# Edge blocks in groups of eight instead of four, six densely summed ranges instead of five, and shorter stages, in a graph network kernel on one core

## The chip, the core and the metric

The kernel runs on one core of a Trainium2 chip. The metric is the device time in microseconds (us) of one execution. The kernel before took 3231.09 us, the median of three runs that lay between 3231.09 and 3231.75 us.

Engines by the names of the profile: PE multiplies matrices and PEld loads its weights, DVE is the vector engine, ACT the scalar engine, POOL is GpSimd, and SP only starts transfers. A q behind a name (SPq) is that engine's own sequencer or transfer queue.

## What is computed

Two layers of a mean-aggregating graph convolution on 12500 nodes with 256 features and 200000 edges, then a third product, the residual and a layer normalization. The edges come sorted by dst, and dst is skewed: it is 12500 times the square of a uniform number, so low node numbers have many edges and high ones few.

```
def _sage_conv(x, src, dst, W_l, b_l, W_r):
    agg = segment_sum(x[src], dst, 12500)
    deg = segment_sum(ones, dst, 12500)
    mean = agg / maximum(deg, 1)[:, None]
    return mean @ W_l + b_l + x @ W_r
h = relu(_sage_conv(x, src, dst, W1_l, b1, W1_r))
h = relu(_sage_conv(h, src, dst, W2_l, b2, W2_r))
out = layernorm(x + h @ W3 + b3)
```

Layer 2 first multiplies h by W2_l and stores the product as z_rows; its gather reads z_rows, as that of layer 1 reads in_x.

## The kernel before, in words

The edges are cut into 1563 blocks of 128. The nodes are cut into 100 ranges of 125 (WN), and the sums of each range have a column block of `acc` in SBUF. Two methods fill the sums.

**Gathered blocks.** All blocks from number 348 (HB) on, 1216 of them, are gathered in each layer: POOL starts one indirect transfer per block (L446), which fetches 128 rows of 256 numbers into `ring`, 4 slots (R) of 4 blocks (GB). For each group of 4 blocks DVE makes a one-hot matrix `oh` by comparing the int16 columns `dcol` with the int16 `iota` (`mark_group`, L1013, 128x500 results), PE multiplies it with the rows (`product`, L538, four products that add into one PSUM bank of three), and DVE adds the bank twice into `acc`, each time with a mask, since a group may touch two neighbouring ranges (`add_masked`, L970). Where a group's node numbers span 125 or more, `later_pass` repeats compare, product and adds; with four blocks no group does. The order of the groups takes one from the low end and one from the high end in turn. POOL waits before the first block of a group for the third product of the group four before it (s_gr), and before its last block for that of the next group.

**Dense ranges.** The first 348 blocks hold nearly all edges of the first 5 (HW) ranges. They aren't gathered. DVE and PE count edges per pair of source and destination node instead: `chunk` makes two one-hot matrices for a pair of blocks (L1063, L1066), PE multiplies them (L589), and DVE copies the counts out (`keep_counts`, L1104). A range has 25 such chunks, and the counts go to HBM (`counts`). Then PE multiplies the counts with all rows of x in 20 steps of 5 products (`dense_step`, L615), and DVE adds two steps at a time to `acc` (`add_hot`, L1120). SP loads counts and rows of each step into two places (`load_step`). A range whose edges lie in the first blocks only in part is also served by `fallback`: 20 steps per layer that load the same rows again and do work only where such a range exists past the dense ones. In this trace none does, and a step there is two small DVE instructions (L1132, L1135), a handshake and its loads.

**Order of the work.** It is written out by hand on each engine, in loops of `four` groups. Layer 1: 4 groups, the table of spans (`spans`), a stage of 48 groups that counts range 0 (a chunk after every second group), four stages of 48 groups that count range w and in their last ten fours run the 20 dense steps of range w-1, two fours with fallback steps, ten fours with the dense steps of range 4, three more fours with fallback steps. Layer 2 has no counting: fallback steps first, then five stages of dense steps, then fours without. Between the groups each finished range of 125 nodes goes through the dense layers (`dense1`, `dense2`, called tiles here), at most one per two groups (`finish_one`). Tables that tell each group's range, offset, passes and finished ranges are computed on DVE, PE and ACT at the start, before the first group.

Of the kernel before, what the change touches and what calls it, by code (L numbers as in the profile page):

```python
# [23 lines left out]
P = 128  # L24
WN = 125
NW = N // WN
GB = 4
# [12 lines left out]
HW = 5  # L40
HB = 348
# [3 lines left out]
C0 = T0 * P  # L45
NC = (NT - T0) * P
G0 = HB // GB
NGG = NG - G0
KJ = (N + P - 1) // P
# [17 lines left out]
TW = 4 * (HW * CH + 1)  # L67
BANKS = 3
STAGE = 48
TAIL_GROUPS = NGG - 4 - STAGE * (HW + 1) - STEPS + 8  # L70
assert STEPS == 4 * PARTS and CD * CH == WN and 2 * FG >= CH and TAIL_GROUPS == 0
# [8 lines left out]
def hot_end(w):  # L80

    return 4 + STAGE * (w + 1) + STAGE

# [18 lines left out]
C_MA = C_BS + HW * CH  # L102
# [7 lines left out]
def constants():  # L110
# [12 lines left out]
    d = np.zeros((HW * CH, D_N), np.float32)  # L123
# [4 lines left out]
    k = np.arange(HW * CH)  # L128
    d[:, D_LIM] = CD * turned
    d[:, D_LIM + 1] = CD * turned + CD - 1  # L130
    d[:, D_LIM + 2] = WN * k
    d[:, D_LIM + 3] = WN * k + WN - 1
# [10 lines left out]
    rows = np.zeros((HW * CH + 1, 4), np.int32)  # L143
# [15 lines left out]
def build(nc, x, src, dst, W1l, b1, W1r, W2l, b2, W2r, W3, b3, c_f, c_s, c_win, c_node, out):  # L159
# [5 lines left out]
    with ExitStack() as ctx:  # L165
# [6 lines left out]
        def sem(name):  # L172
            return ctx.enter_context(nc.semaphore(name))

        acc = sb("acc", [P, (NW + 2) * RW])
        ring = sb("ring", [P, R, GB, RW])
        scol = sb("scol", [P, NC], I32)
        dcol = sb("dcol", [P, NC], I16)
        oh = sb("oh", [P, R, GB, WN])
# [19 lines left out]
        NH = HW * CH  # L199
        tables = sb("tables", [65, NGG * 4], I32)  # L200
        tab = tables[0:1, :]
# [10 lines left out]
        psA, psD = ps4[:, 0:BANKS * 512], ps4[:, BANKS * 512:]  # L212
# [18 lines left out]
        few = scratch[:, u + SJ * WN:u + 2 * SJ * WN].rearrange("p (j n) -> p j n", j=SJ)  # L231
# [4 lines left out]
        cs = scratch[0:NH, u:u + D_N]  # L236
# [10 lines left out]
        span = scratch[0:NH, u:u + 6]  # L247
        u += 6
        m1 = scratch[0:NH, u:u + HB]
# [9 lines left out]

        ident, resid, wt, bs, upper, lower = (cf[:, a:a + n] for a, n in (  # L260
            (C_ID, P), (C_RES, WN), (C_WT, NW), (C_BS, NH), (C_MA, WN + 1), (C_MB, WN + 1)))
# [23 lines left out]
        s_fall = [sem("s_fall0"), sem("s_fall1")]  # L285
# [14 lines left out]
        credit = {s_mm[0]: 4, s_mm[1]: 4, s_ad[0]: 1, s_ad[1]: 1, s_T: 1, s_tc: 1, s_h: 1, s_z: 2,  # L300
# [9 lines left out]
        def _(sp):  # L310
# [17 lines left out]
            tail(1, dst, s_e3)  # L328
            edges(0, src, 0, T0, s_e4)
            sp.dma_start(cs, c_s).then_inc(s_nd, 16)  # L330
            sp.dma_start(iota[:], c_node.to_broadcast([P, NI])).then_inc(s_w, 16)
# [26 lines left out]
            users = [0]  # L358
            last_use = [0, 0]

            def place(q):

# [1078 lines left out]
```

## Time and profile before

| | before |
|---|---|
| median of 3 runs | 3231.09 us |
| the profiled execution's own time | 3232.92 us |
| its span | 3231.0 us |
| PE busy | 2516.2 us (78%) |
| POOL busy | 2368.5 us (73%), 2439 instructions |
| DVE busy | 1483.5 us (46%) |
| ACT busy | 497.8 us (15%) |
| moved by DMA | 651.35 MB, mean 202 GB/s |
| granted PE clock, mean | 0.919 |

The span is what the profiler covers from the first to the last instruction; the execution's own time has 1.9 us around it. POOL is busy for its 2432 gathers and a handful of small instructions. Its busy share is 0.7 to 0.8 of nearly every slice, and the rest of those slices is idle time between two gathers.

### The profile page before, as it was taken

The page shows a single profiled execution, that of the slowest core. Times are in us where ns is not written, and L with a number is a line of the kernel's source. Part 1 is how long each engine was busy: PE and PEld are TensorE (multiplying, and loading weights), DVE is VectorE, ACT ScalarE, POOL GpSimd, SP SyncE. Part 2 cuts the span into 40 slices and gives each one's busy share as a digit, 9 for nine tenths or more (in the row PEclk, how much of TensorE's full clock was granted, in tenths as well). Part 3 has the DMA queues.
Part 4 walks back from the last instruction along what each step waited for, and adds up shares of the span by engine and source line. Part 5 has one row for each costly group of instructions (what it writes and reads, how often), then busy time and mean ns, then how long its engine had stood idle before and what let it go on. Part 6 is the DMA issues. An engine that isn't in the chain of part 4 may idle for free.

```text
span 3231.0 us, 55773 instructions
## 1 busy us (share of the span) xinstructions
PE 2516.2 (78%) x11663; PEld 2060.8 (64%) x11664; DVE 1483.5 (46%) x3552; ACT 497.8 (15%) x1511; POOL 2368.5 (73%) x2439
## 2 busy tenths in 40 slices
PE   4777888888888888687756678878878868877776
PEld 2545677677677677576644556767757757756655
DVE  6777656665655655433333333333333333333332
ACT  2001110101111111110101121112112212211113
POOL 4767777777777777777747777777777777777775
PEclk9989999999999999899978889989989989989978
DMA  4435687687687687777745667757757757757743
GB/s 120 132 115 160 206 251 238 203 254 239 193 256 247 201 255 243 239 219 216 227 147 175 189 193 224 214 169 232 219 171 225 223 171 229 222 174 224 220 121 108
DMA packets 495880, 651.35 MB, mean 202 GB/s; under 512 B 184223, under 2 KB 414230, under 8 KB 492564
## 3 DMA queue, kind: packets, MB, share of 16 engines
q0 software_dynamic: 116736, 318.92, 33.1%
q1 hardware_dynamic: 298228, 254.51, 25.7%
q10 hardware_dynamic: 80800, 76.82, 7.8%
q14 instruction: 98, 0.80, 0.1%
q8 instruction: 18, 0.29, 0.0%
HBM read 579.62 MB, written 70.41 MB: 201 GB/s over the span
## 4 chain that ended last, share of the span: by engine, by line
POOL 40%; issue 20%; PE 19%; DMA 9%; DVEq 7%; DVE 5%; ACT 1%; SPq 0%; ACTq 0%; PEldq 0%; PEld 0%; POOLq 0%
POOL ring L446 40%; PE ps L538 11%; DMA ring<-z_rows,scol 5%; PE ps L615 3%; DMA ring<-in_x,scol 2%; DVEq L990 1%; DVE acc L970 1%; PE psY L659 1%; PE psB L589 1%; DVE oh L1066 1%; DVE oh L1013 1%; PE psY L692 1%; PE psY L648 1%; DVEq L970 1%; PE psT L706 1%
## 5 line engine op out<-in xcount | busy, mean ns | idle before, releaser
L538 PE MATMUL ps<-ring,oh 128*125 128x257 f32 (+1 forms) x4864 | 1332.7, 424 | 547.5 <-DMA ring<-z_rows,scol 286.3
L446 POOL DMA_INDIRECT ring<-in_x,scol x1216 | 1188.1, 977 | 432.1 <-issue 357.7
L538 PEld LDWEIGHTS ps<-ring,oh 128*125 128x125 f32 x4864 | 973.1, 208 | 810.0 <-issue 657.2
L446 POOL DMA_INDIRECT ring<-z_rows,scol x1216 | 1179.8, 970 | 403.6 <-issue 354.3
L970 DVE SCALAR_TENSOR_TENSOR acc<-ps,cf,acc x1224 | 535.6, 479 | 654.4 <-PE ps L538 420.6
L1013 DVE TENSOR_TENSOR oh<-dcol,iota 128x500 f32 x608 | 414.5, 682 | 308.3 <-issue 235.5
L615 PE MATMUL ps<-scratch 128*125 128x257 f32 (+1 forms) x2000 | 490.5, 393 | 11.4 <-DMA scratch<-counts 7.7
L615 PEld LDWEIGHTS ps<-scratch 128*125 128x125 f32 x2000 | 465.6, 296 | 35.0 <-DMA scratch<-counts 8.1
L1363 ACT ACTIVATE work<-psT,b2c 128x125 f32<-128x125 f32 x200 | 62.0, 362 | 1190.5 <-PE psT L710 1190.5
L1327 ACT COPY work<-psY 125x256 f32<-125x256 f32 x100 | 37.2, 372 | 1244.8 <-PE psY L648 1244.8
L589 PE MATMUL psB<-oh 128*128 (+1 forms) x546 | 161.4, 393 | 84.0 <-DVE oh L1066 78.4
L1120 DVE TENSOR_TENSOR acc<-ps,acc 125x256 f32 (+2 forms) x100 | 42.5, 425 | 377.4 <-PE ps L615 364.4
L659 PEld LDWEIGHTS psY<-work,w 128*128 128x128 f32 x1600 | 198.3, 195 | 7.3 <-issue 1.1
L1066 DVE TENSOR_SCALAR oh<-iota,cf,key 128x500 int16 (+1 forms) x546 | 201.1, 410 | 0.0
L659 PE MATMUL psY<-work,w 128*128 128x125 f32 x1600 | 197.7, 277 | 0.8 <-issue 0.8
L589 PEld LDWEIGHTS psB<-oh 128*128 (+1 forms) x546 | 49.7, 97 | 178.0 <-issue 150.8
L648 PE MATMUL psY<-w,hT 128*125 128x256 f32 x400 | 112.5, 406 | 18.4 <-issue 16.9
L706 PE MATMUL psT<-hT,w 128*128 x800 | 121.6, 274 | 0.0
L1063 DVE TENSOR_TENSOR oh<-iota,key 128x256 int16 (+1 forms) x273 | 113.9, 417 | 12.2 <-PE psB L589 10.1
L706 PEld LDWEIGHTS psT<-hT,w 128*128 128x128 f32 x800 | 113.2, 191 | 6.1
L692 PE MATMUL psY<-w,work 128*125 128x256 f32 x400 | 110.6, 401 | 5.3 <-issue 2.8
L1180 DVE RECIPROCAL rs<-sd 125x1 f32 (+1 forms) x100 | 16.4, 164 | 205.5 <-ACT sd L1388 180.0
(139 smaller groups left out, 1211.0 us busy)
## 6 DMA issues: line engine op xcount, KB each, us to landing
scratch<-counts SPq DMA_DIRECT2D x200, 312.5 KB
scratch<-in_x SPq DMA_DIRECT2D x114, 512.0 KB
scratch<-z_rows SPq DMA_DIRECT2D x114, 512.0 KB
counts<-scratch SPq DMA_DIRECT2D x25, 1250.0 KB
work<-in_x ACTq DMA_DIRECT2D x200, 125.0 KB
ring<-in_x,scol POOLq DMA_INDIRECT x1216
ring<-z_rows,scol POOLq DMA_INDIRECT x1216, 3.7
scratch<-in_x SPq DMA_DIRECT2D x114, 128.0 KB
```

The lines of the kernel that those rows point to most:

```text
L446: pool.indirect_dma_start(ring[:, slot, b, 0:D], None, rows_dram, bass.IndirectOffsetOnAxis(scol[:, n - C0:n - C0 + 1], 0)).then_inc(rows[ ...
L538: mm = pe.matmul(psA[0:WN, bass.ds(bank, W)], oh[:, slot, b, :], ring[:, slot, b, 0:W], start=(b == 0), stop=(b == nb - 1))
L589: mm = pe.matmul(psB[:, 0:n], oh1[:, bass.ds(at, P)], oh1[:, bass.ds(at + P, n)], start=first and b == 0, stop=True, skip_group_check=True)
L615: mm = pe.matmul(psD[0:WN, 0:W], lin_a[:, q, :, :, k].rearrange("p f n -> p (f n)"), lin_x[:, q, k, 0:W], start=(q == 0 and k == 0), stop= ...
L648: mm = pe.matmul(psZ[0:WN, 0:D], hT[:, k * WN:(k + 1) * WN], w2[:, k, 0:D], start=(k == 0), stop=(k == 1))
L659: mm = pe.matmul(psH[:, m * WN:(m + 1) * WN], w1[:, a, k, m * P:(m + 1) * P], tT[:, 2 * a + k, :], start=(a == 0 and k == 0), stop=(a == 1 ...
L692: pe.matmul(at, tT[:, k, :], w3[:, k, :], start=(k == 0), stop=False)
L706: pe.matmul(psT[:, m * WN:(m + 1) * WN], w2[:, k, D + m * P:D + (m + 1) * P], hT[:, bass.ds(q + k * WN, WN)], start=(k == 0), stop=False)
L970: ins = v.scalar_tensor_tensor(out=to, in0=psA[0:WN, bass.ds(bank, W)], scalar=mask[0:WN, bass.ds(k, 1)], in1=to, op0=ALU.mult, op1=ALU.add)
L1013: v.tensor_tensor(to, cols, at, ALU.is_equal).then_inc(s_oh[l], 1)
L1063: v.tensor_tensor(s[:, :, 0:P], iota[:, 0:P].unsqueeze(1).to_broadcast([P, 2, P]), key[:, 0, bass.ds(at, 2)].unsqueeze(2).to_broadcast([P, ...
L1066: ins = v.tensor_scalar(s[:, b, P:P + n], iota[:, table:table + n], base, key[:, 1, bass.ds(at + b, 1)], ALU.add, ALU.is_equal)
```

## The change

Groups are 8 blocks (GB = 8, in two ring halves of 4), so each is one compare of 128x1000 results and one pair of masked adds for 8 blocks. The first 376 blocks are not gathered (six dense ranges), which leaves 149 groups, 1192 gathers, per layer. `oh` has 2 buffers of 8 blocks, and `acc` products go to 2 PSUM banks. PE's group is two half products, each waiting for its own 4 blocks, with a dense step placed between the halves. A stage is 11 bodies of two groups. The loop without counts ahead of stage 0 is one body (AHEAD = 1), and no tile is finished in it. The fallback steps (now `general_step`) reuse the rows that the dense steps of the last range (layer 1) or the first range (layer 2) have loaded. The start is reordered: the first group runs before the rest of the tables, the keys and the weight loads.

```
-GB = 4
+GB = 8
+HALF = 4
-HW = 5
-HB = 348
+HW = 6
+HB = 376
-BANKS = 3
-STAGE = 48
+BODIES = NGG // 2
+STAGE = 11
+AHEAD = BODIES - STAGE * HW - 7
-        oh = sb("oh", [P, R, GB, WN])
+        oh = sb("oh", [P, 2, GB, WN])
...
# SP: order at the start, and the loads of the general steps
+            sp.dma_start(cs, c_s).then_inc(s_nd, 16)
+            sp.dma_start(iota[:], c_node.to_broadcast([P, NI])).then_inc(s_io, 16)
...
             edges(0, src, 0, T0, s_e4)
-            sp.dma_start(cs, c_s).then_inc(s_nd, 16)
-            sp.dma_start(iota[:], c_node.to_broadcast([P, NI])).then_inc(s_w, 16)
...
-                if w == HW - 1:
-                    fallback(x, 2, 8)
...
-                    load_step(x, w, t)
+                    load_step(x, w, t, w == HW - 1)
-                if w == HW - 2:
-                    fallback(x, 0, 2)
-            fallback(x, 8, STEPS)
-            fallback(z_dram, 0, STEPS)
# POOL
-                    slot = g % R
                     for b in range(GB):
-                        if g >= R and b == 0:
-                            pool.wait_ge(s_gr[l], g - R + 1)
-                        if g >= R and b == GB - 1:
-                            pool.wait_ge(s_gr[l], g - R + 2)
+                        half, slot = b // HALF, (g + 1) % 2 * 2 + b // HALF
+                        if g >= 2 and b % HALF == 0:
+                            pool.wait_ge(s_gr[l], 3 * (g - 2) + (3 if half else 1))
+                        if g >= 2 and b == HALF - 1:
+                            pool.wait_ge(s_gr[l], 3 * (g - 2) + 2)
+                        if g >= 2 and b == GB - 1:
+                            pool.wait_ge(s_mm[l], credit[s_mm[l]] + g - 1)
# PE
+            def group(l, i, between=()):
...
+                half_product(l, i, 0)
+                for work_ in between:
+                    work_()
+                pe.wait_ge(rows[l][2 * i + 1], landed)
+                half_product(l, i, 1)
...
+                    first_group()
+                    turn_tables()
+                    turn_keys()
...
+                    with pe.Fori(0, AHEAD):
+                        body(finishes=False)
+                    turn_spans()
+                    count()
+                    body(counts=2)
+                    with pe.Fori(0, STAGE - 1):
+                        body(counts=1)
+                    with pe.Fori(1, HW):
+                        count()
+                        body(counts=2)
+                        with pe.Fori(0, STAGE - 1):
+                            body(counts=1, steps=even)
+                    with pe.Fori(0, 3):
+                        body(steps=((0,), (1,)), after=((), (0,)), general=True)
+                        body(steps=((1,), (1,)), after=((0,), ()), general=True)
+                    body(steps=even, general=True)
# DVE
-                mark_group(l, i, nb, off)
+                mark_group(l, i, off)
...
-                add_product(l, i, *(behind[i] if i < 2 else row_of(i - 2)[0:2]))
+                if not first:
+                    add_product(l, 1 - i)
```

On DVE, in the plain groups at the start of layer 1, the rows of one group of four blocks read, with oh the one-hot matrix and acc the sums:

```order
L1013 ISA [waits s_mm0]
L1013 TENSOR_TENSOR oh<-dcol,iota 128x500
L990 ISA
L990 TENSOR_LOAD tables
L976 ISA
L970 ISA [waits s_ad0,s_mm0]
L970 ISA
L970 SCALAR_TENSOR_TENSOR acc<-ps,cf,acc 125x257
L970 ISA
L970 SCALAR_TENSOR_TENSOR acc<-ps,cf,acc 125x257
```

and those of one group of eight blocks:

```order
L1019 ISA [waits s_mm0]
L1019 REGISTER_ALU
L1019 TENSOR_TENSOR oh<-dcol,iota 128x1000
L1051 ISA
L1000 ISA
L1000 TENSOR_LOAD tables
L1001 ISA
L986 ISA [waits s_ad0,s_mm0]
L986 SCALAR_TENSOR_TENSOR acc<-ps,cf,acc 125x257
L986 ISA
L986 SCALAR_TENSOR_TENSOR acc<-ps,cf,acc 125x257
```

The compare has twice the results; the adds keep their size and stand once per eight blocks.

On PE, in a counting stage of layer 1, a group before and the dense step (its operand is scratch) behind it:

```order
L538 ISA [waits s_ad0,s_oh0]
L538 MATMUL ps<-ring,oh 125x257 x4
L543 ISA
L552 TENSOR_LOAD tables
L571 ISA
L604 ISA [waits s_dbank]
L615 MATMUL ps<-scratch 125x257 [waits s_lin0]
L615 MATMUL ps<-scratch 125x257 x4
```

and the same place now:

```order
L543 MATMUL ps<-ring,oh 125x257 [waits s_ad0,s_oh0]
L543 MATMUL ps<-ring,oh 125x257 x3
L607 ISA
L601 ISA [waits s_dbank]
L612 MATMUL ps<-scratch 125x257 [waits s_lin0]
L612 MATMUL ps<-scratch 125x257 x4
L543 MATMUL ps<-ring,oh 125x257 [waits rows0_1]
L543 MATMUL ps<-ring,oh 125x257 x3
```

The dense step has moved from behind a whole group to between its halves.

## Rows read from the trace of the kernel before

**Rows 1.** The costliest groups of the page: line engine op | busy, mean ns | idle before.

```profile
L446 POOL DMA_INDIRECT ring<-in_x,scol x1216 | 1188.1, 977 | 432.1 <-issue 357.7
...
L446 POOL DMA_INDIRECT ring<-z_rows,scol x1216 | 1179.8, 970 | 403.6 <-issue 354.3
L970 DVE SCALAR_TENSOR_TENSOR acc<-ps,cf,acc x1224 | 535.6, 479 | 654.4 <-PE ps L538 420.6
L1013 DVE TENSOR_TENSOR oh<-dcol,iota 128x500 f32 x608 | 414.5, 682 | 308.3 <-issue 235.5
```

**Rows 2.** Line L446: durations ns min/median/max, first and last start, then idle.

```profile
L446 POOL DMA_INDIRECT ring<-z_rows,scol x1216: 942/946/1452, 1654.9 to 3203.8; - x174
...
  issue: 712.0, 2337
```

**Rows 3.** Timeline of POOL, gathers behind a wait: start, us, engine, line [idle before].

```profile
49.62 1.18 POOL L446 DMA_INDIRECT ring<-in_x,scol  x1 [20.31 <-PE ps L538]
...
73.64 0.94 POOL L446 DMA_INDIRECT ring<-in_x,scol  x1 [5.34 <-PE ps L538]
...
190.88 0.94 POOL L446 DMA_INDIRECT ring<-in_x,scol  x1 [14.41 <-PE ps L538]
213.86 1.02 POOL L446 DMA_INDIRECT ring<-in_x,scol  x1 [3.02 <-PE ps L538]
...
1379.31 0.94 POOL L446 DMA_INDIRECT ring<-in_x,scol  x1 [9.54 <-PE ps L538]
...
1620.43 0.94 POOL L446 DMA_INDIRECT ring<-in_x,scol  x1 [3.17 <-PE ps L538]
1654.85 0.94 POOL L446 DMA_INDIRECT ring<-z_rows,scol  x1 [33.48 <-DMA z_rows<-work]
```

**Rows 4.** Timeline of POOL and DVE, three gathers near a compare, in pairs.

```profile
1657.30 0.68 DVE L1013 TENSOR_TENSOR oh<-dcol,iota 128x500 f32 x1 [0.60 <-issue]
1657.35 1.45 POOL L446 DMA_INDIRECT ring<-z_rows,scol  x1 [0.30 <-issue]
...
2630.54 0.95 POOL L446 DMA_INDIRECT ring<-z_rows,scol  x1 [0.31 <-issue]
2630.70 0.68 DVE L1013 TENSOR_TENSOR oh<-dcol,iota 128x500 f32 x1 [0.66 <-issue]
...
2635.29 0.68 DVE L1013 TENSOR_TENSOR oh<-dcol,iota 128x500 f32 x1
2635.54 1.24 POOL L446 DMA_INDIRECT ring<-z_rows,scol  x1 [0.30 <-PE ps L538]
```

**Rows 5.** Timeline of DVE, the widest instruction on two int16 operands, in the preparation.

```profile
33.13 1.43 DVE L877 TENSOR_TENSOR dcol<-dcol,scratch 128x1216 int16<-128x1216 int16 x1 [1.40 <-DMA scratch<-bounds]
```

**Rows 6.** Gathers per 80 us: stretch, length, POOL busy (count), PE clock, DMA share, GB/s.

```profile
0.00:80.00 80.00, 35.05 (x37) 0.91 0.44 120
80.00:160.00 80.00, 61.11 (x63) 0.91 0.44 130
160.00:240.00 80.00, 48.40 (x49) 0.87 0.39 118
240.00:320.00 80.00, 60.80 (x64) 0.98 0.52 158
```

**Rows 7.** Timeline of DVE and PE: first compare, one four of stage 0, its end.

```profile
45.59 0.68 DVE L1013 TENSOR_TENSOR oh<-dcol,iota 128x500 f32 x1 [4.25 <-issue]
...
89.85 0.68 DVE L1013 TENSOR_TENSOR oh<-dcol,iota 128x500 f32 x1 [1.45 <-issue]
...
99.71 3.74 PE L538 MATMUL ps<-ring,oh 128*125 128x257 f32 x16 [0.92 <-DVE oh L1013]
...
109.93 0.68 DVE L1013 TENSOR_TENSOR oh<-dcol,iota 128x500 f32 x1 [1.46 <-issue]
...
330.57 0.68 DVE L1104 COPY scratch<-psB 128x500 f32 x1 [2.11 <-issue]
```

**Rows 8.** All engines, the busiest 80 us of PE: PE, PEld, DVE, ACT, POOL busy.

```profile
480.00:560.00 80.00, 71.90 (x361) 59.73 (x360) 49.89 (x122) 8.81 (x25) 60.80 (x64) 0.98 0.80 252
```

**Rows 9.** Timeline: first dense step of range 4, and the last add of layer 1.

```profile
1372.73 4.66 PE L615 MATMUL ps<-scratch 128*125 128x257 f32 x10 [7.73 <-DMA scratch<-counts]
...
1634.29 0.88 DVE L970 SCALAR_TENSOR_TENSOR acc<-ps,cf,acc  x2 [0.33 <-DVE acc L970]
```

More of the change, by code:

```diff
@@ L781, in layer, with step, body @@
-                with pe.Fori(0, STEPS // 4 + (1 if l else -2)):
-                    four(general=(0, 1, 2, 3) if l == 0 else ())
+                def step(q, general):
+                    dense_step(l, q)
+                    if general:
+                        general_step(l, q)
+                def body(counts=0, steps=((), ()), after=((), ()), general=False, finishes=True):
+                    pe.reg_add(turn, turn, 16 * HALF)
+                    for i in range(2):
+                        group(l, i, [lambda q=q: step(q, general) for q in steps[i]] + [count] * (counts > 1))
+                        for q in after[i]:
+                            step(q, general)
+                        if counts:
+                            count()
+                        if finishes:
+                            finish_one(upto)
@@ L907, in _ @@
-            banks = [v.alloc_register(f"v_bank{k}") for k in range(BANKS)]
-            behind = [[v.alloc_register(f"v_{q}{k}") for q in ("at", "off")] for k in range(2)]
+            rows_at = [[v.alloc_register(f"v_row{k}_{q}") for q in ("w", "off", "passes", "done")] for k in range(2)]
+            behind, ahead = ([v.alloc_register(f"v_{q}_{a}") for a in ("w", "off")] for q in ("behind", "ahead"))
+            c, fin, ga, gb, extra, there, unit, upto = (
+                v.alloc_register(f"v_{q}") for q in ("c", "fin", "ga", "gb", "extra", "there", "unit", "upto"))
@@ L1193, in layer @@
                 v.reg_mov(ga, 0)
-                v.reg_mov(gb, 4 * (NGG - 2))
-                four_rows(front, ga)
+                v.reg_mov(gb, 4 * (NGG - 1))
+                for i in (1, 0):
+                    next_row(i)
                 v.reg_mov(c, 1)
-                for k in range(BANKS):
-                    v.reg_mov(banks[k], k * 512)
                 v.reg_mov(fin, 0)
-                for at, off in behind:
-                    v.reg_mov(at, NW)
-                    v.reg_mov(off, 0)
                 v.reg_mov(at_row, 0)
@@ new lines, in general_body @@
+                def general_body(w, first, second):
+                    for i, turns in enumerate((first, second)):
+                        group(l, i)
+                        for turn in turns:
+                            if turn == "general":
+                                general_step(l)
+                            else:
+                                summed(w)
+                        finish_one(upto)
+                if l == 0:
+                    group(l, 1, first=True)
+                    ends()
+                    keys()
+                    for i in range(2):
+                        v.reg_add((gb, ga)[i], (gb, ga)[i], (4, -4)[i])
+                        next_row(i)
+                    v.wait_ge(s_za, 8)
+                    with v.Fori(0, AHEAD):
+                        body(finishes=False)
@@ L1239, in layer @@
                     hot_chunk()
-                    with v.Fori(0, STAGE // 4):
-                        four(builds=True)
+                    body(counts=2)
+                    with v.Fori(0, STAGE - 1):
+                        body(counts=1)
                     with v.Fori(0, HW - 1) as w:
```

579 lines of the change are left out of this document (277 added, 302 removed).

## The prediction

> **What bounds the kernel now.** I read the page's costliest groups first, then the line of the gathers, then POOL's timeline for every gap over 0.31 us, and last what DVE does around those gaps. PE has the largest busy time, but it isn't the bound. POOL issues 2432 gathers of mean 977 and 970 ns [rows 1], median 946 [rows 2], and nearly every one follows the last after 0.30 us (712.0 us over 2337 gaps) [rows 2]. So a gather costs 1.25 us when nothing disturbs it, and 2432 of them are 3040 of the 3231 us. The reader is to see in the timeline how few real waits there are: 20.3, 5.3, 14.4, 3.0, 9.5 and 3.2 us in layer 1 and none in layer 2, and the 33.5 us between the layers [rows 3]. The rest is 8.9 us ahead of the first gather, 26 us behind the last (3203.8 [rows 2] to 3231.0), and about 70 us in which single gathers take longer than 946 ns: in layer 2, (970 - 946) ns x 1216 = 29.5 us.
>
> What makes a gather longer decides this change. The gather at 1657.35 began 0.63 us before the end of a compare and took 1.45 us; that at 2635.54 began 0.43 us before the end of one and took 1.24; that at 2630.54, in whose course a compare began, took 0.95 [rows 4]. So a gather that starts while DVE compares two int16 operands is held until 0.12 to 0.14 us before the compare's end, and one already running isn't touched. Layer 2 has no counting, so its 29.5 us over 304 compares put at most 0.097 us on a compare.
>
> The Trainium skill (SBUF — State Buffer, section "🔬 SBUF: two separate sides") says that VectorE with two SBUF inputs and GpSimd reading SBUF take an exclusive lock on a shared port pair, for the whole instruction. The trace bears out the hold and not its full extent: the compare at 2630.70 started inside a gather and still took 0.68 us. With the lock held for all of both instructions that compare would have been late; I go by the rows.
>
> **The change part by part.**
>
> Gathers: 1216 become 1192 per layer, 48 fewer at 1.25 us: -60.0 us.
>
> The longer compare: 128x500 takes 0.682 us [rows 1] and 128x1216 on two int16 operands 1.43 [rows 5], so 128x1000 takes 0.68 + 500/716 x 0.75 = 1.20 us. The hold grows faster than the length. If a compare of length T falls at any phase of the 1.275 us that a gather took in layer 2 ((3203.8 - 1654.9)/1215), the mean hold is (T - 0.12)²/(2 x 1.275): 0.123 us at T = 0.68, of which the trace has 79% (0.097), and 0.457 at 1.20, of which 79% are 0.36. I take 0.38. Bounds: 0.17 (growth with the length alone) and 0.46 (all phases alike). Layer 2: 149 compares, and 6 more because six groups of eight blocks span 125 nodes or more (groups 3, 5, 7, 9, 21 and 29 by the sorted dst), 155 x 0.38 = 58.9 against 29.5: +29.4. Layer 1 outside its first stage (there POOL waits for DVE, see below): 125 x 0.38 = 47.5 against 252 x 0.097 = 24.4: +23.1. Together +52.5 us.
>
> Counting: a sixth range has 32 pairs of blocks more (305 against 273), each with a small compare of the same kind; in layer 1 all of them cost (977 - 970) ns x 1216 = 8.5 us, so +1.
>
> The start and stage 0. Here DVE is the bound. One four takes it from 89.85 to 109.93, 20.1 us [rows 7], as long as 16 gathers; stage 0 runs from about 64 to 330.57 [rows 7], 266 us for 12 fours, 25 chunks and the sixteen pairs of the heaviest chunk, which cause the 14.4 us wait. In the new order a group of eight saves DVE one pair of adds (0.88), 0.16 of compare and about 0.2 of gaps, 2.5 us per body; 12 x 2.5 = 30 go, and with 11 bodies instead of 12 another 9 (what is left of a four without its chunks). The 25 chunks stay. New are four second passes in this stage (groups 3, 5, 7, 9): compare 1.2, eight products 3.7 [rows 7], adds 0.9 and handshakes, 7 us each in which DVE waits for PE: +28. Stage 0 thus takes 255 us. It does not begin earlier: the first compare comes at about 35 instead of 45.6 [rows 7], since its table is ready sooner, but then the rest of the tables, keys, one body and the spans follow, and the first chunk comes near 68 (before: 64). So the stage ends near 327, and the next compare lets POOL go on at about 334.5, after 216 gathers, with 976 to go. Before, 37 + 63 + 49 + 64 = 213 gathers were out at 320 [rows 6], 221 at 330.6, and 976 were left at 355. The lead is 20.4 us, where 24 gathers fewer are 30: +9.6. The body with four chunks that opens the next stage takes DVE some 24 us against 21 of POOL: +3. Error of this part by its rough steps: 10 us either way.
>
> Steady stages: before, PE is busy 71.9 of 80 us at its peak and POOL never waits [rows 3, 8]. Ten of eleven bodies instead of ten of twelve fours now carry dense steps; the peak within a body is the same and the slack of POOL is 14 blocks instead of 13. The dense step between the halves is hidden by the wait for the second four gathers (5 us). Cost 0, and 10 to 15 us if the cover goes.
>
> The late waits of layer 1, 9.5 and 3.2: the first came because SP had queued fallback loads ahead of the counts of range 4 [rows 9], and those loads are gone. What is late next is the store and reload of the last range's counts, which PE now meets in the first group after counting: I leave 3 us. -9.
>
> Between the layers: the last add came 13 us after the last gather [rows 3, 9], held up by the fallback handshakes; half a product and one pair of adds take 8. Three tiles still follow, before and now. -5 of the 33.5. The end of layer 2 stays.
>
> Sum: -60.0 + 52.5 + 1 + 9.6 + 3 - 9 - 5 = -7.9 us, against the profiled execution's own 3232.9: 3225.0. It lies 1.8 above the median of the runs, so the time comes to about 3223 to 3225: 3224.
>
> **The rivals.**
>
> A, the hold doesn't grow with the square. If a compare of 1.2 us costs a gather only in proportion (0.17), 280 compares cost 59 us less: 3165. For it: two gathers with a measured relation say nothing beyond 0.68 us. Against: nothing in the rows limits the hold, and 1.08 is still below the period.
>
> B, slower: DVE in stage 0. The second passes make DVE wait for PE while PE's rows, the chunk's banks and the spans wait for DVE. If body 1 with its four chunks and the passes run one after the other with PE at the low clock (eight products at 7 instead of 3.7 us) and the heavy chunk then meets an emptied ring, stage 0 takes 280 to 285 us instead of 255: 3250. It decides from the point at which a body takes DVE more than its 21 us of gathers over several bodies. For it: DVE has no idle in that stage already. Against: the group itself has become cheaper.
>
> C, the dense steps of the last range. 20 steps in 7 bodies instead of 10 fours, some only 5 us apart, with loads of 0.95 MB each, and the reload wait of 7.7 us seen before [rows 9]. If they come late and the shorter rest per stage no longer lets PE catch up, 12 to 16 us: 3238.
>
> D, the start pays off in full: stage 0 costs nothing against before: 3211.
>
> **How the numbers follow.** Forecast 0.50 (own range 3210 to 3240), A 0.15, B 0.20, C 0.10, D 0.05. A measurement of this kernel tells 0.2%, 6.5 us, from no change: faster is below 3224.6, slower above 3237.6. Of the forecast's 0.50, 0.27 is faster, 0.18 the same, 0.05 slower; A and D are faster; B gives 0.17 slower and 0.03 the same; C 0.04 and 0.06. That is 0.47, 0.27, 0.26. The range has to reach halfway into A and to the far side of B: 3178 to 3250.
>
> **What would show it.** In the new profile: 1192 gathers per layer with a median of 946 ns still and a mean near 1000 (970 + 24); compares of 1.20 us; gathers as long as 1.9 us. POOL's waits in layer 1: about 9 and 7 us before 60 us, 30 to 40 us in stage 0, then almost none; layer 2 as long as before, near 1550 us from first to last gather, although it has 24 gathers fewer. It is wrong if the mean gather stays at 975 (A), if the waits before 340 us exceed 75 (B), or if POOL waits in layer 2 at all.

## The result, and the profile of the changed kernel

The changed kernel takes 3302.59 us, the median of four runs (3302.32 to 3305.06), against 3231.09 (four runs beside it, 3229.62 to 3231.75): a ratio of 1.022, 95% interval 1.0206 to 1.0234. The forecast was 3224, range 3178 to 3250. It was wrong, in the sign and by more than its range. The profiled execution took 3302.32 us with a span of 3300.5, 69.5 more than before.

POOL is still the bound. The page's groups, line engine op | busy, mean ns | idle before, against those of [rows 1]:

```profile
L452 POOL DMA_INDIRECT ring<-in_x,scol x1192 | 1197.8, 1005 | 467.4 <-issue 340.3
L452 POOL DMA_INDIRECT ring<-z_rows,scol x1192 | 1184.6, 994 | 419.6 <-issue 343.7
...
L986 DVE SCALAR_TENSOR_TENSOR acc<-ps,cf,acc 125x257 f32 (+1 forms) x620 | 271.9, 480 | 747.7 <-PE ps L543 598.7
L1019 DVE TENSOR_TENSOR oh<-dcol,iota 128x1000 f32 x298 | 359.0, 1205 | 283.3 <-issue 188.2
```

Fewer gathers, but each 24 to 28 ns longer in the mean, and more idle time before them. The two lines of L452 alone, as in [rows 2]: min, median and longest gather, first and last start.

```profile
L452 POOL DMA_INDIRECT ring<-in_x,scol x1192: 940/946/1960, 8.8 to 1665.3; - x199
L452 POOL DMA_INDIRECT ring<-z_rows,scol x1192: 940/946/1975, 1701.4 to 3269.6; - x199
...
  issue: 683.9, 2244
  PE ps L543: 160.4, 138
```

The median is as before and so is the rhythm of undisturbed gathers (946 + 300 ns). The longest is 1.975 us in place of 1.452, which is the longer compare at work. POOL's timeline, gathers behind a wait, against [rows 3]:

```profile
38.55 0.94 POOL L452 DMA_INDIRECT ring<-in_x,scol  x1 [8.66 <-PE ps L543]
...
54.23 0.94 POOL L452 DMA_INDIRECT ring<-in_x,scol  x1 [5.83 <-PE ps L543]
...
88.33 0.94 POOL L452 DMA_INDIRECT ring<-in_x,scol  x1 [14.31 <-PE ps L543]
...
125.83 1.17 POOL L452 DMA_INDIRECT ring<-in_x,scol  x1 [14.21 <-PE ps L543]
...
210.58 0.94 POOL L452 DMA_INDIRECT ring<-in_x,scol  x1 [16.46 <-PE ps L543]
...
1533.01 0.95 POOL L452 DMA_INDIRECT ring<-in_x,scol  x1 [5.04 <-PE ps L543]
...
1577.05 0.94 POOL L452 DMA_INDIRECT ring<-in_x,scol  x1 [7.45 <-PE ps L543]
...
1624.24 0.94 POOL L452 DMA_INDIRECT ring<-in_x,scol  x1 [4.60 <-PE ps L543]
...
1701.38 0.95 POOL L452 DMA_INDIRECT ring<-z_rows,scol  x1 [35.10 <-DMA z_rows<-work]
...
1757.65 0.97 POOL L452 DMA_INDIRECT ring<-z_rows,scol  x1 [4.29 <-PE ps L543]
...
1962.12 0.94 POOL L452 DMA_INDIRECT ring<-z_rows,scol  x1 [6.51 <-PE ps L543]
```

Before, stage 0 had one wait over 6 us (14.4, the heaviest chunk). Now it has three, and layer 2, which had no wait, has waits up to 6.5 us. Gathers per 80 us, against [rows 6]: POOL busy (count), clock, DMA share, GB/s.

```profile
0.00:80.00 80.00, 39.48 (x40) 0.77 0.47 123
80.00:160.00 80.00, 39.90 (x41) 0.87 0.25 71
160.00:240.00 80.00, 43.76 (x45) 0.81 0.40 123
240.00:320.00 80.00, 59.72 (x60) 0.91 0.50 153
```

The second row is where most of it goes: 41 gathers in place of 63. (A gather that lies across the edge of two stretches is counted in both.)

One of the new waits in full, in layer 2, where nothing is counted. PE, DVE and POOL around the second pass of one group (L1027 marks the second window, L535 multiplies it):

```profile
1942.22 1.26 DVE L1027 SCALAR_TENSOR_TENSOR oh<-dcol,cf,iota 128x1000 f32 x1 [1.22 <-issue]
...
1949.77 6.29 PE L535 MATMUL ps<-ring,oh 128*125 128x256 f32 x16 [6.72 <-DMA ring<-z_rows,scol]
...
1956.23 0.88 DVE L986 SCALAR_TENSOR_TENSOR acc<-ps,cf,acc 125x256 f32 x2 [12.76 <-PE ps L535]
...
1957.67 1.20 DVE L1019 TENSOR_TENSOR oh<-dcol,iota 128x1000 f32 x1 [0.56 <-DVE acc L986]
...
1958.92 5.35 PE L543 MATMUL ps<-ring,oh 128*125 128x256 f32 x17 [2.87 <-DVE oh L1019]
...
1962.12 0.94 POOL L452 DMA_INDIRECT ring<-z_rows,scol  x1 [6.51 <-PE ps L543]
```

The marks are ready at 1943.5, but PE waits until all eight gathers have landed. Then its eight products take 6.29 us, DVE adds, marks the group again, and only the product after that frees ring slots. The granted clock of that product (columns: stretch, length, then PE, PEld, DVE, ACT and POOL busy, clock, DMA share, GB/s):

```profile
1949.70:1956.10 6.40, 6.29 (x16) 4.69 (x16) 0.00 (x0) 0.00 (x0) 4.68 (x5) 0.59 0.36 103
```

PE was busy for 7.91 of the 8 us from 1929 to 1937 us, with 1.00 granted. Then it waited 6.7 us, and the products behind that wait run at 0.59 of full speed, near the lower of its two levels (1.2 of 2.4 GHz).

**Where the 69.5 us are.** From all of POOL's gathers I added up, per stretch, what they take over 946 ns ("holds") and the idle time over 0.30 us before them ("waits"). The length of a gather is read to 0.01 us, which makes the holds of a column uncertain by some 2 us. In the last three columns are variants of the experiments below, against the same trace of before.

| us against before | predicted | changed | table in PSUM | one pass | both |
|---|---|---|---|---|---|
| 48 gathers fewer | -60.0 | -60.0 | -60.0 | -60.0 | -60.0 |
| holds, layer 2 | +29.4 | +27.7 | -29.3 | +26.4 | -29.0 |
| holds, layer 1 after 340 us | +24.1 | +30.9 | -18.9 | +28.7 | -19.7 |
| holds and waits before 340 us | +9.6 | +34.6 | +35.2 | +7.1 | -2.3 |
| next stage's first bodies | +3 | +3.5 | +3.4 | 0 | 0 |
| waits after 1300 us, layer 1 | -9 | +6.0 | +12.5 | +5.3 | +11.3 |
| between the layers | -5 | +1.6 | +4.3 | 0 | +3.6 |
| waits, layer 2 | 0 | +21.7 | +21.7 | 0 | 0 |
| after the last gather | 0 | +3.7 | +4.0 | +5.1 | +2.9 |
| span against before, summed | -7.9 | +69.7 | -27.1 | +12.6 | -93.2 |
| span against before, measured | | +69.5 | -27.9 | +12.4 | -94.0 |

### The profile page after: what moved, and what is told of

It is laid out like the page before. It is cut to its first block, busy times and chain, and to the rows that moved or that the text cites. A ratio compares the mean times of both kernels' runs of the same rounds, so it can differ in the third digit from the quotient of the medians.

```text
span 3300.5 us, 51932 instructions
## 1 busy us (share of the span) xinstructions
PE 2632.3 (80%) x12223; PEld 2181.9 (66%) x12224; DVE 1258.8 (38%) x2793; ACT 497.8 (15%) x1514; POOL 2383.0 (72%) x2391
## 3 DMA queue, kind: packets, MB, share of 16 engines
q1 hardware_dynamic: 325202, 273.32, 27.1%
## 4 chain that ended last, share of the span: by engine, by line
POOL 37%; PE 28%; issue 15%; DMA 13%; DVE 4%; DVEq 3%; ACT 0%; SPq 0%; POOLq 0%; ACTq 0%
POOL ring L452 37%; PE ps L543 14%; DMA ring<-z_rows,scol 6%; PE ps L612 5%; DMA ring<-in_x,scol 4%; PE psY L653 3%; PE ps L535 2%; PE psB L586 2%; PE psY L642 2%; DVE oh L1019 1%; DVE oh L1068 1%; DMA scratch<-in_x 1%; DMA counts<-scratch 1%; PE psT L668 1%; PE psY L686 0%
## 5 line engine op out<-in xcount | busy, mean ns | idle before, releaser
L543 PE MATMUL ps<-ring,oh 128*125 128x257 f32 (+1 forms) x4768 | 1292.9, 420 | 492.8 <-DMA ring<-z_rows,scol 303.4
L452 POOL DMA_INDIRECT ring<-in_x,scol x1192 | 1197.8, 1005 | 467.4 <-issue 340.3
L452 POOL DMA_INDIRECT ring<-z_rows,scol x1192 | 1184.6, 994 | 419.6 <-issue 343.7
L543 PEld LDWEIGHTS ps<-ring,oh 128*125 128x125 f32 x4768 | 950.5, 206 | 729.2 <-issue 302.0
L612 PE MATMUL ps<-scratch 128*125 128x257 f32 (+1 forms) x2400 | 592.4, 395 | 20.8 <-DMA scratch<-counts 13.4
L612 PEld LDWEIGHTS ps<-scratch 128*125 128x125 f32 x2400 | 561.2, 296 | 49.5 <-DMA scratch<-counts 13.8
L986 DVE SCALAR_TENSOR_TENSOR acc<-ps,cf,acc 125x257 f32 (+1 forms) x620 | 271.9, 480 | 747.7 <-PE ps L543 598.7
L1019 DVE TENSOR_TENSOR oh<-dcol,iota 128x1000 f32 x298 | 359.0, 1205 | 283.3 <-issue 188.2
L586 PE MATMUL psB<-oh 128*128 (+1 forms) x610 | 185.2, 402 | 66.9 <-DVE oh L1068 59.5
L1122 DVE TENSOR_TENSOR acc<-ps,acc 125x257 f32 (+3 forms) x120 | 51.1, 426 | 475.1 <-PE ps L612 467.3
L1068 DVE TENSOR_SCALAR oh<-iota,cf,key 128x500 int16 (+1 forms) x610 | 223.5, 409 | 0.0
L1106 DVE COPY scratch<-psB 128x500 f32 x150 | 101.8, 679 | 55.4 <-issue 22.4
```

The costliest lines, as they stand in the source:

```text
L452: pool.indirect_dma_start(ring[:, slot, b % HALF, 0:D], None, rows_dram, bass.IndirectOffsetOnAxis(scol[:, n - HB:n - HB + 1], 0)).then_in ...
L543: mm = pe.matmul(psA[0:WN, i * 512:i * 512 + W], oh[:, i, b, :], ring[:, 2 * i + half, b % HALF, 0:W], start=(b == 0), stop=(b == GB - 1))
L586: mm = pe.matmul(psB[:, 0:n], oh1[:, bass.ds(at, P)], oh1[:, bass.ds(at + P, n)], start=first and b == 0, stop=True, skip_group_check=True)
L612: mm = pe.matmul(psD[0:WN, 0:W], lin_a[:, q, :, :, k].rearrange("p f n -> p (f n)"), lin_x[:, q, k, 0:W], start=(q == 0 and k == 0), stop= ...
L986: ins = v.scalar_tensor_tensor(out=to, in0=psA[0:WN, i * 512:i * 512 + W], scalar=mask[0:WN, bass.ds(k, 1)], in1=to, op0=ALU.mult, op1=ALU ...
L1019: v.tensor_tensor(to, cols, at, ALU.is_equal).then_inc(s_oh[l], 1)
```

## The experiments

Eighteen runs were made, in five groups. Three groups (names beginning p, q and d) fell on chips on which the kernel before takes 3847.9, 3843.2 and 3890.9 us. Their times are read only against their own runs of before and against each other. The groups c and e ran where the kernel before takes 3234.0 and 3232.1 us.

**The table of places in PSUM (p1, q1, d1, e1).** The compare's second operand is copied once to PSUM, into the bank between `psA` and `psD`, and read there.

```
+        psP = ps4[:, 2 * 512:2 * 512 + 2 * WN]
...
+            link(v.tensor_copy(psP, iota[:, CJ + FN:CJ + FN + 2 * WN]))
...
-                return iota[:, bass.ds(v.snap(off, min_val=1, max_val=WN) + (CJ + FN), WN)]...
+                return psP[:, bass.ds(v.snap(off, min_val=1, max_val=WN), WN)]...
```

> The changed kernel with the position table of the compare copied once to PSUM, so that the compare has one operand in SBUF instead of two. Theory 'two SBUF operands hold the gather': of the 131 us by which gathers exceed 946 ns, all but the counting part (about 10 to 15 us) go, the mean gather falls from 1005 and 994 ns to under 960, and the time falls from 3302 by 100 to 120 us to about 3190; a little less, since in stage 0 POOL waits for DVE anyway. Rival 'any long DVE instruction on int16 holds it': the excess stays near 131 us and the time near 3302.

> The table of places in PSUM alone, for the corner between the changed kernel (3299) and the one without holds and second passes (3141). Theory (the costs add): if this chip takes about 3234 us for the kernel before, 3302 - 112 and 10 back as waits: 3190 to 3200, ratio 0.987 to 0.990. Rival (what the holds give goes into waits at the second passes): above 3215. On a chip that takes 3850 or more for the kernel before: 0.990 again.

Measured on the chip of 3232 us (e1): 3198.97, ratio 0.9896 (0.9876 to 0.9916). It is 1.0% below the kernel before, and 100 us below the changed kernel (c1, on another chip of that kind). The gathers of e1:

```profile
L453 POOL DMA_INDIRECT ring<-in_x,scol x1192: 940/946/1812, 8.7 to 1622.2; - x199
L453 POOL DMA_INDIRECT ring<-z_rows,scol x1192: 940/946/1057, 1660.9 to 3171.9; - x199
```

In layer 2 no gather is longer than 1.057 us, where the changed kernel had 1.975. The compare itself hardly changed:

```profile
L1021 DVE TENSOR_TENSOR oh<-dcol,ps 128x1000 f32 x298 | 356.5, 1196 | 283.7 <-issue 182.5
```

So what holds the gather isn't the compare's length alone but that both its operands lie in SBUF. One by one: in the changed kernel 199 gathers start at least 0.06 us after a compare's start and 0.14 us before its end, and all 199 are held; in e1 221 do, and none is. The masked adds, with one operand in PSUM and one in SBUF, hold none in either. Holds fall from 131.1 to 19.8 us (-111.3), waits rise from 118.6 to 130.1: the time falls by what the theory said, and the rival (all turns into waits) is out. What is left is in layer 1 and is mostly the counting's: 5.7 us behind its TENSOR_TENSOR (L1067), which reads two operands from SBUF, and 8.6 us behind its TENSOR_SCALAR (L1070), which reads one table from SBUF, a number per partition, and writes SBUF. So two SBUF operands aren't the only form that holds a gather. On the slow chips the same edit gave 0.9923 (0.9897 to 0.9948), 0.991 (0.9884 to 0.9936) and 0.9894 (0.9872 to 0.9917), with holds of 19.0, 14.2 and 21.6 us.

**Two compares of 500 (p4).** One more look at the hold: the same work as two 128x500 instructions.

```
-                v.tensor_tensor(to, cols, at, ALU.is_equal).then_inc(s_oh[l], 1)
+                for h in range(2):
+                    part_ = slice(h * GB // 2, (h + 1) * GB // 2)
+                    ins = v.tensor_tensor(to[:, part_, :], cols[:, part_, :], at[:, part_, :], ALU.is_equal)
+                ins.then_inc(s_oh[l], 1)
```

> The changed kernel with each 128x1000 compare cut into two of 128x500 back to back. Theory 'a waiting gather gets in between two compares, so the hold goes with the square of the length': the excess falls from 131 us to about 70 (2 x 0.097 per group), time 3302 - 50 to 60 = 3247. Rival 'the hold goes with the total compare time, since the second compare begins before the gather does': the excess stays at 131 us or grows, and DVE has 0.16 us more per group: 3302 to 3310.

Measured: 3815.28 at 3847.92 before, ratio 0.9907 (0.988 to 0.9935); holds 68.6 us, where p3 on the same chip, with compares of 1000, has 102.7. One pair in the timeline of p4:

```profile
2310.66 1.27 DVE L1021 TENSOR_TENSOR oh<-dcol,iota 128x500 f32 x2 [0.72 <-issue]
2311.57 1.18 POOL L452 DMA_INDIRECT ring<-z_rows,scol  x1 [0.30 <-issue]
```

The gather starts 0.36 us before the end of the pair and takes 0.23 longer than 0.95; the hold lasts to 0.13 us before the compare's end, as in [rows 4]. With the 19.0 us taken off that p1, on the same chip, has without this compare, halving the instruction brings 83.7 to 49.6, a factor of 0.59. Growth with the length alone gives 1 (two of half the length), growth with the square of what lies above 0.12 us gives 2 x (0.51/1.08)² = 0.45. It lies between, nearer to the square. Counted by the compares alone (the excess of the gathers that start within one), 87.2 us in p3 become 43.7 in p4, a factor of 0.50. And the trace shows how: a gather that starts in the first of the two is let go before the second.

```profile
2037.07 1.27 DVE L1021 TENSOR_TENSOR oh<-dcol,iota 128x500 f32 x2 [1.06 <-issue]
2037.17 1.40 POOL L452 DMA_INDIRECT ring<-z_rows,scol  x1 [0.30 <-issue]
```

It is held for 0.45 us, until 0.13 us before the end of the first compare (0.68 us long); held to the end of the pair it would have taken 1.99. So the theory stands and its rival is out.

**One pass for every group (p2, q2, e2).** The edges in the second window of the six groups that span 125 nodes or more are left out.

```
-                 v.tensor_scalar(sent[:, 4, :], more_l, 1.0, None, ALU.add))
+                 v.tensor_scalar(sent[:, 4, :], more_l, 0.0, 1.0, ALU.mult, ALU.add))
```

> The changed kernel with the number of passes set to one for every group; it leaves out the edges of six groups that fall past their first 125 nodes. Theory 'the second passes cost the waits': layer 2's waits (21.7 us of POOL) go entirely, and of the 61 us of stage 0 about 25 to 30, plus 7 of the two at 323 and 408 us; time 3302 - 50 to 60 = about 3245. Rival 'stage 0 is short of DVE whatever the passes, and layer 2 waits for the split groups': at most 10 us go, 3292.

> One pass for every group alone (edges of six groups left out), for the fourth corner. Theory (the costs add): 3302 - 50 = 3252 where the kernel before takes 3234, ratio 1.004 to 1.007, no waits in layer 2 and 45 us in stage 0. Rival (second passes are hidden while the holds stretch the gathers): above 3285. On a chip that takes 3850 or more for the kernel before: 0.971 again.

Measured (e2, chip of 3232 us): 3252.33, ratio 1.0062 (1.0043 to 1.0081), as expected. POOL's timeline of e2, its longest waits behind 60 us:

```profile
77.44 0.94 POOL L452 DMA_INDIRECT ring<-in_x,scol  x1 [5.02 <-PE ps L543]
...
181.31 1.00 POOL L452 DMA_INDIRECT ring<-in_x,scol  x1 [12.22 <-PE ps L543]
...
1501.11 0.94 POOL L452 DMA_INDIRECT ring<-in_x,scol  x1 [6.03 <-PE ps L543]
...
1544.06 0.94 POOL L452 DMA_INDIRECT ring<-in_x,scol  x1 [6.52 <-PE ps L543]
...
1665.93 0.94 POOL L452 DMA_INDIRECT ring<-z_rows,scol  x1 [33.51 <-DMA z_rows<-work]
```

In stage 0 one wait over 6 us is left, the heaviest chunk's, and none in layer 2. The waits fall from 118.6 to 60.5 us, so twelve second passes cost 58.1 us of waits, 4.8 each, while the holds stay at 132.4. The span falls by 57.1 us. The late waits of layer 1 stay too; they have another cause. On the slow chips the ratios were 0.9705 (0.9667 to 0.9743), 0.9711 (0.9677 to 0.9744) and, in d2, 0.9718 (0.9694 to 0.9743): 74, 73 and 73 us below the table in PSUM on the same chip. There the order of the two edits is reversed: on the chip of 3232 us the table in PSUM is 53 us below one pass.

**The other corners (c1, c3, c4), and before once more (c2).** c1 is the changed kernel again, c2 the kernel before.

> The changed kernel itself, as the control for the variants of it. If this chip takes 3231 us for the kernel before, 3302 again, ratio 1.022. If it takes 3845: the holds cost what they did, near 130 us over 946 ns, against 19 with the table in PSUM; the waits of POOL would be smaller than the 460 and 277 us of the table in PSUM by what the holds take, so the ratio lies at 0.990 to 1.000, and the second passes (against the variant without them, 0.9705) cost 70 to 110 us.

> The kernel before, with every group of four blocks given one pass (edges of the groups that span 125 nodes or more are left out). Theory: the second passes of the changed kernel are new, six groups of eight against one or two groups of four, so nearly nothing changes here: ratio 0.995 to 1.000, where the same edit of the changed kernel takes 2 to 3%. Rival: the second passes cost the kernel before as much, 0.97 to 0.98, and are no cause of the difference.

> Both suspected costs taken from the changed kernel: the table of the compares in PSUM, and one pass for every group (edges of six groups of eight left out). Theory (two separate costs): on a chip that takes 3231 for the kernel before, 3302 - 112 - 50 = 3140; on one that takes 3845, where POOL waits for DVE and PE anyway, what the holds give back goes into waits and the time is within 15 us of the variant with one pass alone, 0.967 to 0.972. Rival: the holds count there too, 0.94 to 0.95.

c1: 3298.56, ratio 1.0191 (1.0169 to 1.0213), nearly the waits of the trace above (94.0 and 23.6 us in the two layers, against 96.9 and 21.7). c2: 3234.87, waits of 50.3 us in layer 1 (54.1 in the trace shown) and none in layer 2; it is a single run, and it fell on a chip of the faster kind, so its expectation of 600 us of waits was not put to the test. c3: 3232.91, ratio 0.9999 (0.9989 to 1.0009): the kernel before has no group that needs a second pass (no instruction of that path is in its trace), so the edit gives nothing and its rival is out. c4, both edits: 3140.8, ratio 0.9716 (0.9693 to 0.9739); 3140 was expected. From c1, the table in PSUM gives 100 us, one pass 46 (both measured on the chip of 3232 us), and both edits 158. The two costs are separate, and nearly add up: both together give 12 us more than the sum, little above the noise of four medians. In c4 the gathers of layer 2 run undisturbed:

```profile
L453 POOL DMA_INDIRECT ring<-z_rows,scol x1192: 942/946/1072, 1617.4 to 3106.9; - x199
```

**What in a second pass costs (d3).** With the table in PSUM, the wait for the second four gathers is put into the middle of the pass's products.

```
-                pe.wait_ge(rows[l][2 * i + 1], landed)
                 pe.wait_ge(s_ohx, marked)
                 pe.wait_ge(s_ad[l], cv)
                 for b in range(GB):
+                    if b == HALF:
+                        pe.wait_ge(rows[l][2 * i + 1], landed)
```

> The table in PSUM, and the product of a second pass waits for the second four gathers in its middle instead of before its first block. Theory (half of a pass's cost is that its eight products begin only when the eighth gather has landed): 2 us less in each of the twelve passes, 15 to 25 us less than the table in PSUM alone. Rival (DVE's queue sets the pass: it cannot compare again before the pass's add): within 6 us of the table in PSUM alone.

Measured: 3858.46, ratio 0.991 (0.9882 to 0.9938), against 3853.07 of d1 on the same chip: no gain, as the rival said. Its waits are 483.4 and 297.6 us against 464.7 and 291.4. But it ran only on a slow chip, so for a fast one this stays open.

**The code of the general steps (p3, d4).** With this input no edge needs the general steps, and both engines jump over their bodies. p3 leaves the bodies out of the changed kernel, d4 out of the one with the table in PSUM.

```
-                 with pe.If(HW < end):
-                     with pe.Fori(HW, end):
...
-                 with v.If(HW < end):
-                     with v.Fori(HW, end) as w:
...
```

> The changed kernel without the body of the general steps (it never runs with these inputs: no range past the dense six has edges in the first 376 blocks); handshakes and the two small DVE instructions stay. Theory 'the late waits of layer 1 are the dense steps of the last range and the reload of counts': nothing changes, 3302 within 3 us. Rival 'they are code being fetched on the jump back of a long loop' (DVE idles 7.0 us for nothing the profile shows before 1572.6): POOL's 7.5 us wait at 1577 and perhaps those after it go, 8 to 15 us, 3290.

> The table in PSUM, and the bodies of the general steps, which both engines jump over with this input, left out of the program. Theory (the jumps and the long loops of these bodies cost): the two waits late in layer 1 that follow a gap of DVE without a releaser (7.3 and 4.3 us in the variant with one pass and the table in PSUM) go, and part of the 37 us between the layers: 10 to 15 us less than the table in PSUM alone; the wait on the reload of the last range's counts (7.5) stays. Rival (they come from the reload alone): all stay, within 4 us.

p3: 3807.75, ratio 0.9903 (0.987 to 0.9935). d4: 3846.86, ratio 0.9883 (0.9861 to 0.9905), 6 us below d1 with intervals that overlap. So the times are inconclusive: on these chips late waits can't be told from others.

The traces do settle one part. In every run that keeps the bodies and has six dense ranges, the layer-1 compares number 140 and 144 start after DVE has stood for 4.8 to 7.8 us with no releaser in the trace. In d4, which has no bodies, the same two compares:

```profile
1871.84 1.20 DVE L1008 TENSOR_TENSOR oh<-dcol,ps 128x1000 f32 x1 [1.44 <-issue]
...
1919.12 1.20 DVE L1008 TENSOR_TENSOR oh<-dcol,ps 128x1000 f32 x1 [1.40 <-issue]
```

In p3 they are 2.40 and 1.42 us. The bodies cost DVE some 5 us twice, though it never enters them.

**Five dense ranges (q3), dense steps behind the group (q4).** q3 keeps groups of eight, with HW = 5 and HB = 344. q4 is the table in PSUM with the dense step moved from between the two half products to behind both.

```
-                for work_ in between:
-                    work_()
                 pe.wait_ge(rows[l][2 * i + 1], landed)
                 half_product(l, i, 1)
+                for work_ in between:
+                    work_()
```

> The changed kernel with five dense ranges (HW = 5, HB = 344): 1224 gathers per layer instead of 1192, and 14 bodies ahead of stage 0 instead of 1, so the four second passes fall ahead of the counting; last range's dense steps still in 7 bodies. Theory 'passes and counting collide in stage 0': of POOL's 97 us of waits in layer 1 some 45 go; 64 gathers more are 80 us, their compares 3; 3302 + 83 - 45 = 3340. Rival 'the waits belong to counting alone': they stay at 90 or more, 3380.

> As q1_psum, and each dense step (and the second pair of counts) behind the whole group instead of between its halves. Theory 'the place between the halves hides the step': POOL's waits grow by 5 to 20 us against q1_psum. Rival 'it is the place between the halves that delays the product and with it the next compare and the late waits of layer 1 (20 us)': the waits shrink by 5 to 15 us. No difference would say that ring slack covers either.

q3: 3823.97, ratio 0.9946 (0.9927 to 0.9966), with 64 gathers more than the changed kernel; for lack of the changed kernel on that chip it says nothing of the sixth range's worth. q4: 3990.78, ratio 1.040 (1.0355 to 1.0445), 184 us over q1. There the place between the halves hides the steps, as its theory said, by far more than its 5 to 20 us. On these slow chips POOL waits anyway, so 184 is not its price on the others.

## Why the prediction was wrong

**What was right.** The bound (POOL, 1.25 us per undisturbed gather), the 60 us of gathers, and the hold. The price of 0.38 us per compare gave +53.5 us with the counting's 1, and +58.6 came; in layer 2 it is 59.2/155 = 0.382. The growth was argued from two durations and three gathers, and e1 and p4 show the mechanism. The prediction scaled its formula by 79% to meet the trace; the trace says where most of that comes from. A gather that starts from 0.05 us before to 0.04 us after a compare's start isn't held, and the compare is up to 0.08 us longer instead (0.755 and 1.269 us at most). A gather is held if it starts 0.045 us or more into the compare and 0.127 or more before its end. By these figures (T - 0.17)²/(2 x period) gives an estimate of 0.10 and 0.40 us per compare, where 0.10 and 0.38 were measured. The Trainium skill (SBUF — State Buffer, section "🔬 SBUF: two separate sides") says that VectorE takes the shared pair with two SBUF inputs; e1, with one input in PSUM, agrees (2.2 us of holds in layer 2 for 59.2). Rival A (no growth beyond the length) is out, and so is D.

Two slips in the working change little. The parts of the chances add up to 0.25 for the same and 0.28 for slower, where 0.27 and 0.26 stand. And 213 gathers at 320 us counts those across the edges of [rows 6] twice: it was 210, so 976 were left at 360 us and not at 355, and the term of +9.6 should have been about +4.

**What failed, first: the saving in stage 0.** The prediction took DVE to be the bound there ("DVE has no idle in that stage already") and let 30 + 9 us go for what groups of eight save it, enough to pay for 28 us of second passes. The rows of the kernel before don't bear that out. The four of [rows 7] takes 20.1 us, but its 16 gathers alone take 20.0, and the engines in that stretch (length, then PE, PEld, DVE, ACT and POOL busy, clock, DMA share, GB/s) are:

```profile
90.00:110.00 20.00, 14.54 (x57) 9.48 (x56) 15.09 (x39) 0.58 (x1) 15.13 (x17) 0.89 0.38 106
```

DVE is busy for 15.1 of 20 us, and POOL has no wait. POOL's waits in the whole stage are 22.0 us (mainly the 5.3, 14.4 and 3.0 of [rows 3]), so no more than that could be saved. e2 shows what came. Without any second pass the holds and waits before 340 us are +7.1, where +9.6 was forecast with four; the waits from 60 to 340 us are 30.3 us. The 217th gather starts at 335.5 us, where POOL was to go on at 334.5 with the passes. In the changed kernel it starts at 364.0, 28.5 us later for four passes. So the 28 us were about right, and what was to pay for them didn't come: +38.1 in place of +12.6 with the bodies behind, an error of 25.5. Why the waits of the stage rose from 22.0 to 30.3 with less work on DVE isn't shown; the ring now holds two groups where it held four, and no run separates that.

Rival B has the size: 26 us above the forecast, and its sign, more than 75 us of waits before 340 us, came at 75.4. The clock was as low as it said (0.57 from 64 to 90 us, 0.76 before). But it made the second passes dearer than 28 us, and taking them away gives back 28, so its number is in part luck. The +3 for the first body of the next stage is luck too: +3.5 came, as the wait for a second pass at 408 us, and without the passes it is 0.

**Second: the second passes in layer 2, nothing against +21.7.** The prediction counted a compare each there and no stall. The trace shows 6.7 us of waiting for eight landings, 6.3 us of products at the lower clock granted after this wait, the add, the compare again: DVE stood for 12.8 us. And a ring of 16 gathers, two groups, lets POOL go on for only 20 us, so with one group held it runs dry also where the engines have slack. Taking the passes away takes 58.1 us of waits: 32.3 before 340 us (75.4 against 43.1), 3.5 at 408 us and 21.7 in layer 2. The sentence "if POOL waits in layer 2 at all" named the sign, but no term and no rival priced it.

**Third: the late waits, -9 against +6.0.** The queue of SP no longer has fallback loads ahead, but the reload of the last range's counts took their place, and cost more than the 3 us left for it. The timeline of the changed kernel, SP's queue, PE and POOL:

```profile
1515.12 16.29 SPq L390 DMA_DIRECT2D scratch<-counts  x3
...
1526.36 4.66 PE L612 MATMUL ps<-scratch 128*125 128x257 f32 x10 [13.39 <-DMA scratch<-counts]
...
1533.01 0.95 POOL L452 DMA_INDIRECT ring<-in_x,scol  x1 [5.04 <-PE ps L543]
```

PE waits 13.4 us where it waited 7.7 before [rows 9]; POOL's wait for it is 4.7 us over its 0.3, where 3 was left. The rest is another thing: DVE stops for 7 us, released by nothing that the trace shows.

```profile
1572.59 1.20 DVE L1019 TENSOR_TENSOR oh<-dcol,iota 128x1000 f32 x1 [7.02 <-issue]
1573.84 3.06 PEld L543 LDWEIGHTS ps<-ring,oh 128*125 128x125 f32 x8 [5.92 <-DVE oh L1019]
...
1577.05 0.94 POOL L452 DMA_INDIRECT ring<-in_x,scol  x1 [7.45 <-PE ps L543]
```

It comes twice, at 1572.6 and 1619.8 (7.12), 47 us apart, before compares number 140 and 144. One pass through the loop with the general bodies has four compares, and its three passes have two jumps back. Without the bodies the stops are gone (d4 and p3, above), so they belong to this long loop; that it is code fetched on the jump back is only argued. POOL's waits behind them are 7.2 and 4.3 us over the 0.3. The kernel before has gaps of 7.5 and 6.8 us like them (1590.7 and 1616.4), with one wait of 2.9 us behind [rows 3]: the gaps aren't new, only what they cost. Rival C again has the size, 12 to 16 us above the forecast where 15.0 came, but its cause, the late steps and the reload, has 1.7 of them and the stops of DVE 11.4.

**Fourth: between the layers, -5 against +1.6, and the end, 0 against +3.7.** "Three tiles still follow, before and now" is wrong: four follow the last add now, in both places. From the last add to the first gather of layer 2 it takes 23.5 us where it took 19.7, and from the last add to the end 24.8 where it took 20.7. The last add of layer 1 comes 11.6 us after the last gather, between the 8 forecast and the 13.8 of before.

With the measured sizes in place of these terms (+5.1 holds, +25.5 stage 0 and the bodies behind it, +15.0 late waits, +6.6 between the layers, +21.7 layer 2, +3.7 end) the -7.9 becomes +69.7. The two largest parts of the 77.6 us are the saving that stage 0 couldn't give and the second passes of layer 2.

## What to carry to other kernels

Time saved on an engine is worth no more than the waits of the bound engine in that stage. Here one four took as long as its 16 gathers, 22 us of waits stood in the stage, and 39 us of saving were forecast. Add up the bound engine's waits there first.

A path that the code takes rarely (here 12 passes beside 298 regular ones) is priced by how long it keeps the buffer that the bound engine refills, not by the busy time of its instructions: add the wait for its inputs, its work at the clock granted after that wait, and every handshake until the first slot comes free. Larger groups can create such a path: of 304 groups of four none needed it, of 149 groups of eight six did. And where short GpSimd-issued gathers are the bound, look at which VectorE instructions read two operands from SBUF: moving one small table to PSUM took 111 us of holds away and turned a kernel 2% slower than before into one 1% faster.

## What the runs showed of the hardware

- A gather that starts while a VectorE TENSOR_TENSOR reads two SBUF operands is held until 0.12 to 0.14 us before that instruction's end. The hold is 0.38 us in the mean for an instruction of 1.205 us, and under 0.02 (2.2 us over 155 compares) with one operand in PSUM, at 1.196 us. A TENSOR_SCALAR that reads a table from SBUF and writes SBUF holds gathers too, though not all (69 of 93 that start inside one of the counting's in the changed kernel).
- The other way round the cost is small: only a gather that starts within 0.05 us of the compare's start delays it, by up to 0.08 us. The 195 compares that start later than that inside a running gather all take their usual time (1.203 us at most).
- A compare cut into two back to back lets a waiting gather through between them (p4: 43.7 us of holds for 87.2).
- The same kernel takes 3231 to 3235 us on some chips and 3843 to 3891 on others. An undisturbed gather costs 1.25 us on both, and POOL waits 756 us in d1 where it waits 130 in e1, the same kernel. What causes it stays open. Releasers are hard to read in these traces, since part of the semaphore records is missing (d1 has 380 updates of one PE semaphore, e1 448). A ratio from such a chip didn't carry over to the others: one pass for every group gave 0.972 there and 1.006 here.
